# Audio tower on one core: constants waited for in two steps, late expert weights loaded by SyncE, stage orders of all engines laid out anew

## What is computed

```python
h = tok(x)        # depthwise conv of 7 taps, 192x192 product, relu, max over pairs (125 -> 62), real(fft2), layer norm
h = h + attn0(layernorm(h))   # 8 heads of 64/96, relative positions: rel = q @ r_k, shifted row by row, added to the scores
h = h + ffn0(layernorm(h))    # weights rounded to -1, 0, 1; activations rounded to 8 bits; silu(gate) * up; down
h = h + attn1(layernorm(h))   # 12 heads of 16 with 3 key heads, rotary positions, window mask
h = h + moe(layernorm(h))     # 8 experts, the best one for each token: silu(x @ w1[e]) * (x @ w2[e]) @ w3[e], times its probability
```

## Time and profile before

| | us |
|---|---|
| median of three runs (1203.88 to 1205.45) | 1205.06 |
| the profiled execution, its own time | 1207.81 |
| its span, first to last instruction | 1205.9 |
| start, iterations up to n = 4, to about | 130 |
| 27 periods of the full pipeline | 748.8 |
| drain, from the last full iteration to the first expert product | about 141 |
| expert phase | 185.6 |
| busy: PE, ACT, DVE, POOL | 1004.8, 838.8, 792.0, 368.1 |

### The profile page before, as it was taken

How to read it: one execution, slowest core, us unless ns; L and a number is a source line. 1 busy time by engine, 2 the same in 40 slices (tenths; PEclk the granted TensorE clock), 3 DMA queues, 4 the chain that set the end, 5 groups by cost and what they waited for, 6 DMA issues and landing times. The chain is left out here.

```text
span 1205.9 us, 31213 instructions
## 1 busy us (share of the span) xinstructions
PE 1004.8 (83%) x9406; PEld 761.8 (63%) x9439; DVE 792.0 (66%) x2641; ACT 838.8 (70%) x2673; POOL 368.1 (31%) x1100
## 2 busy tenths in 40 slices
PE   3658988999899999898998999999888541999996
PEld 2436666666666666666666666666666421888885
DVE  2355777777777777777777777777775422555553
ACT  1436888888888888888888888888887420333332
POOL 2012333333333333333333333333332211122222
PEclk9987999999999999999999999999999655999998
DMA  6135111111111111111111111111111007122221
GB/s 217 33 118 156 33 40 39 38 45 38 38 38 55 43 48 38 38 38 38 39 43 38 38 44 49 48 43 38 38 33 33 12 20 212 49 58 56 56 61 39
DMA packets 73487, 65.62 MB, mean 54 GB/s; under 512 B 39341, under 2 KB 63696, under 8 KB 73328
## 3 DMA queue, kind: packets, MB, share of 16 engines
q1 hardware_dynamic: 63232, 46.43, 12.9%
q0 software_dynamic: 4512, 12.52, 3.2%
q10 hardware_dynamic: 5712, 6.29, 1.8%
HBM read 36.57 MB, written 28.95 MB: 54 GB/s over the span
## 5 line engine op out<-in xcount | busy, mean ns | idle before, releaser
L1192 DVE SCALAR_TENSOR_TENSOR conv_lo<-xT_lo,c_taps,conv_lo 128x248 f32<-128x248 f32 x192 | 89.8, 468 | 20.4 <-ACT xT_hi L901 20.4
L1137 ACT ACTIVATE e_tanh<-bank_a 128x512 f32<-128x512 f32 x34 | 20.3, 597 | 93.4 <-PE bank_a L590 93.4
L1087 ACT ACTIVATE p<-bank_b,max 128x62 f32<-128x62 f32 x384 | 81.1, 352 | 0.0
L499 POOL TENSOR_TENSOR var_y<-ssq_y,c_eps 128x1 f32<-128x1 f32 x32 | 6.1, 192 | 235.3 <-ACT f_sq L1057 235.3
L590 PE MATMUL bank_a<-e_xT,w_now 128*128 128x128 f32 x544 | 70.5, 284 | 7.5 <-DVE e_gate L1467 3.4
L590 PEld LDWEIGHTS bank_a<-e_xT,w_now 128*128 128x128 f32 x544 | 64.9, 196 | 16.7 <-issue 11.0
L590 PE MATMUL bank_a<-c_wv,a_xT 64*64 64x384 f32 (+1 forms) x512 | 74.0, 503 | 0.0
L590 PE MATMUL bank_a<-a_xT,c_wq 64*128 64x128 f32 (+1 forms) x512 | 71.7, 282 | 0.0
L1462 DVE COPY w_now<-w_sb 128x512 f32 x34 | 14.5, 427 | 83.9 <-PE bank_a L590 74.6
L590 PE MATMUL bank_a<-a_xT,c_wk 64*128 64x128 f32 (+1 forms) x512 | 69.2, 281 | 0.0
L590 PE MATMUL bank_a<-c_wo,oT 128*128 128x192 f32 x384 | 68.5, 329 | 0.5 <-ACT oT L901 0.4
(11 more groups left out here) (264 smaller groups left out, 3006.7 us busy)
## 6 DMA issues: line engine op xcount, KB each, us to landing
rel_scores<-rel_tok SPq DMA_DIRECT2D x32, 492.0 KB, 2.6
rel_skew<-rel_scores SPq DMA_DIRECT2D x64, 124.0 KB, 3.0
x_tok<-in_x SPq DMA_DIRECT2D x32, 187.5 KB
e_rest<-routed SPq DMA_DIRECT2D x34, 97.0 KB
e_tok<-routed SPq DMA_DIRECT2D x34, 96.0 KB, 1.9
routed<-pad_rows SPq DMA_DIRECT2D x8, 386.0 KB, 2.8
w_sb<-in_w ACTq DMA_DIRECT2D x1, 3072.0 KB, 12.4
w_sb<-in_w ACTq DMA_DIRECT2D x2, 1024.0 KB, 14.7
```

What stands on the lines that cost most here:

```text
L499: pool.tensor_tensor(out=var[k][:, :], in0=ssq[k][:, :], in1=c_eps[:, width:width + 1], op=ALU.mult).then_inc(var_eps[k], 1)
L1087: last = nc.scalar.activation(p1[:, h, 0:T], src[:, at * T:(at + 1) * T], ACT.Exp, bias=max1[:, mx:mx + 1])
L1137: nc.scalar.activation(e_tanh[:, :], pa0[:, :], ACT.Tanh, scale=0.5).then_inc(e_tanhr, 1)
L1192: c.mark(v.scalar_tensor_tensor(conv_lo[:, :, :], xT_lo[:, :, k:k + PAIRS], c_taps[:, 0, k:k + 1], conv_lo[:, :, :], ALU.mult, ALU.add))
```

## The change

1. *Constants.* `ident` counts with `x_loaded`, so the first `t_transpose` waits for `ident` and `x_tok` alone. `c_gamma`, `c_beta` and `c_feat` move from `w_t` to `w_a`; the five constants left in `w_t` are waited for in `t_pointwise`, `t_middle_tap` and by DVE. `rk` goes to bank b0. ACT's sums of absolute weights, a stage `sum_weights` now, stand behind the first `t_copy_z`; PE's part stands before the first `a_relative`. ACT's `prepare` is behind the copies of `a_copy_x`.
2. *Late weights.* SP issues them when `a_project_v` of the last tile is done, before the padding. POOL only marks them.
3. *Padding.* SP no longer waits for the scatters ahead of the last before it writes the padding.
4. *Orders.* All four tables are new.

```diff
-            sp.dma_start(ident[:, :], ident_in).then_inc(w_t, 16)
+            sp.dma_start(ident[:, :], ident_in).then_inc(x_loaded, 16)
...
+            sp.wait_ge(a_v, 4 * TILES)
+            for e, landed in w_late.items():
+                load_weights(sp, slice(e, e + GE), landed)
             sp.wait_ge(pads_ready, 1)
             sp.wait_ge(pads_placed, 1)
-            sp.wait_ge(r_scattered, 16 * (TILES - 1))
...
-            pool.wait_ge(r_scattered, 16 * TILES)
-            for e, landed in w_late.items():
-                load_weights(pool, slice(e, e + GE), landed)
...
+            mark_weights(w_early, range(EARLY))
+            pool.wait_ge(r_scattered, 16 * TILES)
+            for e, landed in w_late.items():
+                mark_weights(landed, range(e, e + GE))
...
-                pe.wait_ge(x_loaded, 16 * m + 16)
+                pe.wait_ge(x_loaded, 16 * m + 32)
...
             def t_pointwise(m):
+                if first(m):
+                    pe.wait_ge(w_t, LOADS_T)
...
             def a_relative(m):
+                if first(m):
+                    sum_weights()
...
-            pe.wait_ge(w_t, LOADS_T)
             overlapped(pe, (
-                (1, t_transpose), (3, a_output), (2, a_project), (4, b_transpose), (4, b_project), (2, a_relative),
+                (4, f_down), (1, t_transpose), (3, a_output), (2, a_project), (4, b_transpose), (4, b_project),
...
                 copy(z_sb[:, :], pt[:, 0:D]).then_inc(t_zs, 1)
+                if first(m):
+                    sum_weights()
             def a_copy_x(m):
-                if first(m):
-                    prepare()
...
             overlapped(act, (
-                (2, a_copy_x), (1, t_middle_tap), (1, t_copy_x), (4, b_normalise_in), (3, f_normalise_in),
+                (3, a_copy_heads_hi), (3, a_copy_heads_lo), (2, a_copy_x), (1, t_middle_tap), (1, t_copy_x),
```

More of the change, by code:

```diff
@@ L387, in _ @@
             sp.dma_start(c_dft_seq[:, :, :], dft_seq).then_inc(w_t, 16)
[L388 to L390 removed]
+            sp.dma_start(c_gamma[:, :], bass.AP(gamma.tensor, 0, [[0, P], [1, D]])).then_inc(w_a, 16)
+            sp.dma_start(c_beta[:, :], bass.AP(beta.tensor, 0, [[0, P], [1, D]])).then_inc(w_a, 16)
+            sp.dma_start(c_feat[:, :], rk_feat).then_inc(w_a, 16)
             sp.dma_start(c_wrk[:, :], wrk).then_inc(w_a, 16)
@@ L563, in _, with mark_weights @@
             overlapped(pool, (
-                (4, f_dequant_x), (3, a_keep), (4, f_inv_sqrt_y), (2, t_inv_sqrt), (2, t_scale), (6, r_scatter),
-                (4, f_dequant_y), (4, f_scale), (3, a_scale), (3, f_inv_sqrt_x), (5, b_scale)))
-            pool.wait_ge(r_scattered, 16 * TILES)
-            for e, landed in w_late.items():
-                load_weights(pool, slice(e, e + GE), landed)
-            for landed, es in ((w_early, range(EARLY)), *((landed, range(e, e + GE)) for e, landed in w_late.items())):
+                (3, a_keep), (6, b_scale), (4, f_inv_sqrt_x), (4, f_dequant_x), (4, f_inv_sqrt_y), (2, t_inv_sqrt),
+                (2, t_scale), (4, f_dequant_y), (6, r_scatter), (4, f_scale), (3, a_scale)))
+            def mark_weights(landed, es):
                 pool.wait_ge(landed, 64)
@@ L603, in prepare, with sum_weights @@
                 for hp in range(HP):
-                    last = mm(pa0[:, hp * REL:(hp + 1) * REL], c_wrk[:, hp * P:(hp + 1) * P], c_feat[:, :])
+                    last = mm(pb0[:, hp * REL:(hp + 1) * REL], c_wrk[:, hp * P:(hp + 1) * P], c_feat[:, :])
                 last.then_inc(rk_done, 1)
+            def sum_weights():
+                pe.wait_ge(rk_stored, 1)
                 pe.wait_ge(wabs, 2)
@@ L854, in r_rank @@
                 mm(pa0[:, TT:TT + NE + 1], ones16[:, :], chosen[:, :]).then_inc(r_ranked, 1)
-            pe.wait_ge(w_t, LOADS_T)
             overlapped(pe, (
-                (1, t_transpose), (3, a_output), (2, a_project), (4, b_transpose), (4, b_project), (2, a_relative),
[L859 to L863, removed]
+                (4, f_down), (1, t_transpose), (3, a_output), (2, a_project), (4, b_transpose), (4, b_project),
+                (2, a_relative), (1, t_pointwise), (4, b_transpose_qk), (2, a_project_v), (3, f_transpose_x),
+                (4, b_scores), (3, f_project_up), (5, r_transpose), (3, f_project_gate), (2, a_scores),
+                (2, a_add_relative), (1, t_dft), (5, r_route), (1, t_dft_seq), (4, b_probs_transpose),
+                (2, a_probs_transpose), (5, r_rank), (4, b_values), (2, a_values), (4, b_transpose_o),
+                (3, f_transpose_y), (4, b_output), (2, a_transpose_heads), (1, a_transpose)))
             def e_transpose(j):
@@ L910, in prepare, with sum_weights @@
                 act.wait_ge(cleared, 3)
-                copy(rk[:, :, :].rearrange("p h r -> p (h r)"), pa0[:, 0:HP * REL]).then_inc(rk_stored, 1)
+                copy(rk[:, :, :].rearrange("p h r -> p (h r)"), pb0[:, 0:HP * REL]).then_inc(rk_stored, 1)
+            def sum_weights():
                 act.wait_ge(w_f, LOADS_F)
@@ L957, in a_copy_x @@
                 copy(a_xT[KB:P, 1, :], pa0[0:KB, P:2 * P]).then_inc(a_xTr, 1)
+                if first(m):
+                    prepare()
             def a_bias_qw(m):
@@ L1114, in _ @@
             overlapped(act, (
-                (2, a_copy_x), (1, t_middle_tap), (1, t_copy_x), (4, b_normalise_in), (3, f_normalise_in),
[L1116 to L1121, removed]
+                (3, a_copy_heads_hi), (3, a_copy_heads_lo), (2, a_copy_x), (1, t_middle_tap), (1, t_copy_x),
+                (4, b_normalise_in), (4, b_copy_x), (2, a_copy_k), (3, f_normalise_in), (4, b_copy_v),
+                (3, f_square_x), (2, a_copy_rel_even), (2, a_copy_rel_odd), (5, r_normalise_in), (2, a_bias_qw),
+                (4, b_copy_q), (3, f_round_x), (5, r_keep), (3, f_copy_x), (2, a_copy_v0), (1, t_relu),
+                (2, a_copy_v1), (5, r_copy_x), (3, f_tanh_gate), (4, b_expo), (1, t_copy_z), (3, f_square_y),
+                (2, a_expo), (4, b_copy_probs), (2, a_copy_probs), (3, f_round_y), (5, r_expo), (4, b_copy_o),
+                (3, f_copy_y), (1, a_normalise_in)))
             def e_copy_x(j):
@@ L1219, in t_moments @@
                 ch["t"].stage("moments", m)
+                if first(m):
+                    dve.wait_ge(w_a, LOADS_A)
                 dve.wait_ge(t_y, m + 1)
@@ L1419, in _ @@
             overlapped(dve, (
[L1420 to L1423, removed]
+                (4, f_residual), (3, a_residual), (1, t_convolve_1), (2, a_bias_q), (1, t_convolve_2), (4, b_rotate),
+                (3, f_quantise_x), (4, b_key_blocks), (1, t_pool), (4, b_max_scores), (3, f_silu), (2, a_max_scores),
+                (5, r_choose), (5, r_choose_one), (1, t_moments), (3, f_quantise_y), (4, b_normalise), (1, t_norm),
+                (2, a_normalise), (5, r_slots), (4, b_residual)))
             n_plan = [n_setup[0]]
```

4 lines of the change are left out of this document (2 added, 2 removed).

## The result

The changed kernel takes 1194.93 us (median of 4 runs, 1193.70 to 1195.41), the kernel before took 1204.47 beside it (4 runs). The ratio is 0.9918, 95% interval 0.9904 to 0.9932: **9.5 us faster**, where 23.65 were forecast, and 0.9 us outside the range. The profiled execution took 1195.02, its span is 1193.2.

| stretch | before | after | difference | predicted |
|---|---|---|---|---|
| start, to the first transposition of `a_in` | 33.56 | 27.85 | -5.71 | -5.8 |
| to the last transposition of `a_in`, 31 iterations | 872.74 | 883.17 | **+10.43** | -4.3 |
| drain, to the last transposition of `b_in` | 62.46 | 58.51 | -3.95 | -2.4 |
| to the first padding transfer | 24.29 | 20.95 | -3.34 | -3.75 |
| to the issue of `e_tok` | 17.91 | 18.10 | +0.19 | 0 |

A forecast was written before the change was run, and what follows sets the result against it. PE was taken to bound the full pipeline, with short waits for ACT. The terms -5.8, -4.3, -2.4, -3.75 and -7.4 sum to -23.65, so 1205.06 - 23.65 = 1181.4 us, range 1173 to 1194.

The forecast's parts named there:

- The start: Up to the first transposition of `a_in`: constants and moved absolute sums save 6.2 us, net -5.8, bounds -3 and -6.5.
- the 0.4 against it: Start: tile 0's `t_dft` now stands behind `a_add_relative`'s wait for its transfer; between 0 and 1.6, taken as 0.4 us.
- One period: Full pipeline: 0.11 lost and 0.27 gained give -0.16 us per period, times 27 = -4.3; called the least certain term.
- DVE's detour over `r_route`: Each period: `r_route` ends 0.61 later behind `t_dft`, so DVE chooses later and passes +0.11 us on to `f_yq`.
- PE has work until it reads either: nothing: ACT's middle of each period: new order puts `f_xq` at PE's need and `rel_tok` 0.3 later, costing nothing.
- slower than before: Rival, full pipeline: PE, DVE and ACT wait if `rel_skew` is late in each tile; 1218 at 1.5 later; chance 0.03.
- the transfer was steady: Argument against PE waiting for `rel_skew`: landed by 534.3, asked at 534.90, and the same in all periods looked at.
- the period does not shrink: Rival, full pipeline: `r_route` path or `z_sb`'s wait eats the gain; 0 to +0.3 per period, 1189 us, chance 0.24.
- The drain: Last tiles: `b_output` ahead of `f_down` shortens DVE's wait of 2.89; between 0 and 2.89, taken as -2.4 us.
- The turn: Between drain and experts: padding starts earlier, -3.75 us; `e_tok` lands without late weights beside it, -7.4 us.
- The late weights did not hit the last tile: Rival, drain: late weights slow the last `rel_skew` to 9.3 us, PE waits some 6; 1187.4 us, chance 0.09.
- The expert phase: After the turn: the expert phase itself keeps its length, predicted difference 0.

The follow-up runs named there:

- ACT's old middle: Changed kernel with ACT's stages from `b_normalise_in` to `f_copy_x` in the order of the kernel before; `a_add_relative` keeps its new place: ratio 0.9878.
- `a_add_relative` last: Changed kernel with `r_route` and `t_dft` ahead of `a_add_relative` on PE again, and DVE's choice ahead of `a_max_scores`: ratio 0.988.
- the one with both edits: Changed kernel with `a_add_relative` behind `r_route` and `t_dft`, DVE's choice ahead of `a_max_scores`, and ACT's `b_normalise_in` to `f_copy_x` in the old order: ratio 0.9845.
- the kernel before with SP's stages swapped: Kernel before with only SP's `t_load_x` (load of the next tile's `x_tok`) put ahead of `a_skew`: ratio 0.9991.

## Why the prediction was wrong

**The start was right** in its size, -5.71 against -5.8, by some luck. At the first transposition of `a_in` the working has -6.2; the 0.4 against it comes later. So 0.5 is missing. `c_dft_seq` landed 4.2 behind its issue, at 7.6, not 7.3, and the first convolution began at 8.00 because ACT's table load stood in front of it, 6.71 to 7.99. In the kernel before this load lay at 0.71, and the forecast has no term for it. Behind that transposition nothing was lost: PE's wait for tile 0's `rel_skew` grew from 1.65 to 2.58, but the stretch up to the fourth `a_in` got 0.66 shorter, and why was not taken apart. The absolute sums lay from 23.18 to 26.0, as worked out; ACT was then idle until 27.25, when `norm_shift_t` came from POOL.

**One period was wrong: +0.39 instead of -0.16.** Its parts, measured in a period without the wait for `rel_skew` (`a_in` at 658.35):

```profile
659.48 2.22 PE L593 MATMUL bank_a<-c_wo,oT 128*128 128x192 f32 x12
668.44 1.05 ACT L910 ACTIVATE rel_tok<-bank_a 128x492 f32<-128x492 f32 x2
674.88 1.07 PE L593 MATMUL bank_a<-kBD,qw 128*64 128x124 f32 x16
683.32 0.72 ACT L1055 ACTIVATE f_yq<-f_gate,magic 128x512 bf16<-128x512 f32 x1
687.24 1.57 PE L593 MATMUL bank_a<-c_wo,oT 128*128 128x192 f32 x8
```

and the same instructions in the kernel before, one period:

```profile
657.43 2.12 PE L590 MATMUL bank_a<-c_wo,oT 128*128 128x192 f32 x12
665.78 1.05 ACT L901 ACTIVATE rel_tok<-bank_a 128x492 f32<-128x492 f32 x2
672.57 1.07 PE L590 MATMUL bank_a<-kBD,qw 128*64 128x124 f32 x16
```

- From the end of `f_yq` (684.04) to `a_output` (687.24): 3.20, forecast 3.17, before 3.44. The new end of the body does what was said.
- DVE's detour over `r_route`, forecast +0.11: from `a_scores` to the end of `f_yq` it is 9.16 in both kernels (684.04 - 674.88; before, 681.73 - 672.57). Nothing.
- From `a_output` to `a_scores`, forecast nothing: 674.88 - 659.48 = 15.40 against 672.57 - 657.43 = 15.14. **+0.26.** "PE has work until it reads either: nothing" is the step that failed. 0.10 of it is in `a_output` itself (2.22 instead of 2.12), and stays with ACT's old middle. The rest goes with ACT's middle: its copy of `vBD` starts 7.60 behind `a_output` instead of 7.40, so `q_rot` and `k_rep` come late, and `f_xq` ends when PE could have taken it. The run with ACT's old middle has 15.24 here, and its least period is lower by 0.17; with `a_add_relative` last as well it is 15.14 again.
- These three make 27.75, the least period of the changed kernel, where 27.57 was forecast: the gain of the end was spent in the middle.
- `rel_tok` starts 668.44 - 659.48 = 8.96 behind `a_output` instead of 8.35: 0.6 later, where I had said 0.3.
- The wait for `rel_skew`, the other 0.37. The mechanism stands in the forecast as the rival "slower than before", with a spare of 0.3 and a chance of 0.03. **The step that failed is the spare and the reason given for it: "the transfer was steady".** The landing "by 534.3" was at 534.64; with `rel_tok` 0.3 later that is 534.94, and PE asks at 534.90, so even in the one period that I read no spare was left. The time from issue to need was worked out well, 3.8 against 3.77. The spread, 2.7 to 4.2 a read, was one view away in the trace of before, and with it the spare is negative in half of the tiles. The price comes to 0.37 a tile on average, half of the 0.7 at which the kernel would have been slower.

So "the period does not shrink" was too mild: it allowed up to +0.3.

**The drain** gave 3.95 instead of 2.4. The forecast took it from DVE's wait of 2.89 for `b_output`. In the changed kernel this wait is 1.69, 1.2 less:

```profile
965.64 0.35 DVE L1392 TENSOR_TENSOR res_m<-res_b,bank_b 128x192 f32<-128x192 f32 x1 [1.69 <-PE bank_b L593]
```

The other 2.7 came earlier in the drain. TensorE's granted clock differs there from run to run: it changes between its levels of 2.4 and 1.2 GHz where PE has less to do (39.57 us of 58.51 here, 692.63 of 759.32 in the pipeline, where it stays up). The changed kernel, then the one with late weights on POOL, then the one with both edits:

```profile
911.02:969.53 58.51, 39.57 (x314) 27.97 (x315) 29.91 (x105) 35.02 (x115) 17.30 (x58) 0.81 0.29 78
```

```profile
916.59:976.71 60.12, 42.12 (x316) 29.81 (x315) 29.93 (x105) 35.05 (x115) 17.30 (x58) 0.77 0.07 23
```

```profile
898.76:961.71 62.95, 43.36 (x317) 30.35 (x315) 30.04 (x106) 34.94 (x115) 17.44 (x58) 0.73 0.26 72
```

Mean clock 0.81, 0.77 and 0.73, length 58.5, 60.1 and 63.0. The kernel before and the one with the three changes and the old orders took 62.5 and 62.4 at 0.76, so against the run nearest in clock the new order is worth 2.3, about the forecast. But the kernel before with SP's stages swapped took 61.8 at 0.74, less than the 63.0 beside it. So how much of the 3.95 is the order and how much the clock is not shown; no run held the clock.

**The turn** was right: -3.34 and -7.31 against -3.75 and -7.4; SP takes 1.66 from the start of `pads_at` to the first transfer, not 0.17. The late weights did not hit the last tile: their loads were issued from 926.1, just behind the last `rel_skew`, which landed in 3.5 us (median of its two reads), as in the kernel before.

**The expert phase**, forecast unchanged, was 3.0 shorter. No run ties this to the change. A step takes 4.90 us, but now and then 5.47; here is PE at two steps of the run with `a_add_relative` last, 5.46 apart:

```profile
1044.07 0.44 PE L596 MATMUL bank_t<-ident,e_tok 128*128 128x128 f32 x2
1049.53 0.44 PE L596 MATMUL bank_t<-ident,e_tok 128*128 128x128 f32 x2
```

Its profiled execution had nine such steps of 33, the kernel before two, the changed one none. Those two and a first step of 6.42 instead of 7.22 make 2.0 of the 3.0, and the stretch behind the last transposition 1.0.

## What to carry to other kernels

Before an order brings forward the reader of a transfer, read the slowest landing of that transfer over all iterations and set it against the time from issue to need; a median or one period does not show it, and once the spare is gone the pipeline waits for the slow ones only. Take the landing itself from the trace: a wait read as a length has to be added to the moment at which it began, and 0.3 us lost there was all the spare. Ask then what else is in flight: moving an unrelated load away from the transfer cost nothing and brought back nine of the ten us. And a reordering whose parts are each worth 0.1 to 0.3 a period has to be counted over the whole loop body: the stretch that I had written off as free took back what the other gained.

## What the runs showed of the hardware

- Two transfers of one queue, 187.5 KB issued 0.2 us behind 2 x 124 KB, stretch the landing of the first: up to 4.1 us instead of 3.2, at a mean DMA share of 0.13. How much it is changes from tile to tile with nothing in the program that changes. With the load moved away, and ACT's old middle, one read of 52 still took 3.8.
- A stretch with such waits does not repeat: 783.8 to 791.3 us in four executions, where the even ones of two kernels agree to 0.1.
- Steps of the expert phase are 0.57 longer at times, none to nine in one execution, up to 5 us together. The cause was not sought.
